# State-space scan: the rows of C by way of memory and a broadcasting transfer instead of a product and a copy

## The reference

```python
x_dbl = einsum('bld,ed->ble', x, W_xproj)          # 64 + 16 + 16 columns
dt_low, Bm, Cm = split(x_dbl, [64, 80])            # Bm, Cm: 16 values per token
delta = softplus(einsum('blr,dr->bld', dt_low, W_dt) + b_dt)
# for each of 256 channels d and 16 states n, along the 128 tokens t:
h[t, d, n] = exp(delta[t, d] * A[d, n]) * h[t-1, d, n] + delta[t, d] * x[t, d] * Bm[t, n]
y[t, d]    = sum_n h[t, d, n] * Cm[t, n]
x = layernorm(x + y)
```

## Time and profile before

| what | value |
|---|---|
| median of 3 runs | 1385.7 us (1383.73 to 1385.78) |
| profiled execution, its own time | 1390.1 us |
| span of the profiled execution | 1388.3 us |
| mean granted clock of TensorE | 0.929 of full |
| scan phase | from the start to about 522 us |
| VectorE busy from 30 to 507.3 us | 460.1 of 477.3 us |
| TensorE busy in the same stretch | 366.4 us |
| ScalarE | 298.5 us |
| GpSimd | 336.7 us |
| transfers in the same stretch | 2% of 16 DMA engines, 7 GB/s |

### The profile page before, as it was taken

How to read it: one execution, slowest core, us unless ns; L and a number is a source line. 1 busy time by engine, 2 the same in 40 slices (tenths; PEclk the granted TensorE clock), 3 DMA queues, 4 the chain that set the end, 5 groups by cost and what they waited for, 6 DMA issues and landing times. The chain is left out here.

```text
span 1388.3 us, 25930 instructions
## 1 busy us (share of the span) xinstructions
PE 1079.9 (78%) x8527; PEld 733.4 (53%) x8527; DVE 1000.8 (72%) x1898; ACT 751.8 (54%) x1601; POOL 794.1 (57%) x730
## 2 busy tenths in 40 slices
PE   5877778787777766888888888213999999999980
PEld 1332323233232224666666666103899989999970
DVE  2999999999999984787787776574455555555534
ACT  4666575666657624666667665202555555555433
POOL 2686776768677654777777775403144644454423
PEclk8999999999999997999999998556999999999995
DMA  3000000000000001111111100203134444434227
GB/s 108 16 16 1 16 0 15 1 15 15 0 1 0 1 0 33 37 35 42 38 34 43 38 31 33 77 0 110 55 66 108 97 104 72 107 84 79 42 22 254
DMA packets 43463, 64.01 MB, mean 46 GB/s; under 512 B 8288, under 2 KB 34592, under 8 KB 41248
## 3 DMA queue, kind: packets, MB, share of 16 engines
q1 hardware_dynamic: 31104, 46.11, 10.0%
q0 software_dynamic: 12288, 17.05, 7.5%
HBM read 42.00 MB, written 21.14 MB: 45 GB/s over the span
## 5 line engine op out<-in xcount | busy, mean ns | idle before, releaser
L514 POOL TENSOR_TENSOR scan_hc<-scan_state,scan_c_sb 128x1024 f32<-128x1024 f32 x128 | 305.4, 2391 | 142.8 <-DVE scan_state L442 132.9
L442 DVE TENSOR_TENSOR_SCAN scan_state<-scan_decay,scan_drive_ps 128x512 f32<-128x512 f32 x256 | 297.7, 1205 | 0.2
L223 PE MATMUL scan_y_ps<-scan_hc,all_ident 128*128 128x512 f32 x520 | 256.6, 617 | 3.1 <-POOL scan_hc L514 3.1
L1662 DVE TENSOR_TENSOR expert_hid_lo<-expert_hid,expert_hid_hi 128x512 fp32r<-128x512 f32 x128 | 88.6, 692 | 176.6 <-ACT expert_hid_hi L1646 163.4
L1559 POOL DMA_INDIRECT acc<-expert_rows,expert_lst x64 | 113.0, 1766 | 179.5 <-DVE expert_rows L1688 163.1
L1641 ACT ACTIVATE expert_hid<-expert_h_ps,expert_b 128x512 f32<-128x512 f32 x128 | 88.3, 690 | 199.0 <-PE expert_h_ps L556 175.8
L326 ACT ACTIVATE scan_decay<-scan_delta,scan_a_neg 128x508 f32<-128x508 f32 x256 | 169.6, 716 | 7.4 <-POOL scan_delta L496 7.2
L435 DVE TENSOR_TENSOR scan_drive_ps<-scan_dx,scan_b_ps 128x512 f32<-128x512 f32 x256 | 162.6, 681 | 14.3 <-POOL scan_dx L501 10.3
L368 ACT ACTIVATE scan_c_sb<-scan_c_ps 128x512 f32<-128x512 f32 x128 | 76.6, 599 | 138.7 <-PE scan_c_ps L216 129.6
L556 PE MATMUL expert_o_ps<-weights_w_hi,expert_hid_lo 128*128 128x256 f32 x512 | 143.2, 280 | 0.0
L223 PEld LDWEIGHTS scan_y_ps<-scan_hc,all_ident 128*128 128x128 f32 x520 | 99.8, 197 | 82.0 <-issue 72.7
(11 more groups left out here) (221 smaller groups left out, 2452.9 us busy)
## 6 DMA issues: line engine op xcount, KB each, us to landing
weights_w<-w SPq DMA_DIRECT2D x16, 1024.0 KB
table<-all_row SPq DMA_DIRECT2D x32, 132.0 KB, 1.8
scan_xT<-xT SPq DMA_DIRECT2D x8, 512.0 KB, 4.0
attn_ctxT<-ctxT SPq DMA_DIRECT2D x32, 128.0 KB, 2.4
acc<-all_row SPq DMA_DIRECT2D x32, 128.0 KB, 1.7
final_a<-acc SPq DMA_DIRECT2D x8, 512.0 KB, 6.5
out<-final_o SPq DMA_DIRECT2D x8, 512.0 KB, 4.2
expert_b<-b SPq DMA_DIRECT2D x8, 128.0 KB, 3.0
```

Source lines behind the costliest of these rows:

```text
L223: last = pe.matmul(y_ps[k][:], ident[0][:], hc[:, n % RING, k, :], start=False, stop=(n == NS - 1))
L442: dve.tensor_tensor_scan(state[:, n % RING, k, :], decay[:, n % RING, k, :, :].rearrange("p b t -> p (b t)"), drive_ps[k][:], 0.0, ALU.mul ...
L514: pool.tensor_tensor(hc[:, n % RING, :, :], state[:, n % RING, :, :], c_sb[:, n % RING, :].unsqueeze(1).broadcast_to([P, KH, GT]), ALU.mul ...
L1662: dve.tensor_tensor(hid_lo[:, f % RING_H, :], hid[:, f % 2, :], hid_hi[:, f % RING_H, :].bitcast(F32), ALU.subtract).then_inc(hid_ready, 1)
```

## The change

The rows of C are no longer spread by a product. ScalarE makes one more copy per group, of the 32 raw rows of B and C in fp32 (`c_rows`), directly behind the first bf16 part. SP stores C's 16 rows of 512 values (32 KB) to a buffer in memory, `c_dram`, one of two. Then for each step SP issues a transfer that reads one row of 2 KB and writes it to all 128 partitions of a slot of `c_sb` (256 KB), three steps ahead of the step that uses it. `broadcast_c`, its PSUM tile and ScalarE's copy are gone. GpSimd waits for the transfer, with a semaphore per slot of the ring. The semaphore `bc_high` is replaced by `c_rows_ready`, which comes after the fp32 copy, for both who waited for it: `split` on VectorE and `step_size` on TensorE. SP's program is written out by step, in a loop over pairs of groups: the store of the next group's rows stands at n = 12, and the load of xT moves to n = 14.

```diff
+                def store_rows(i, par):
+                    g = 2 * i + par
+                    sp.wait_ge(c_rows_ready, g + 1)
+                    sp.dma_start(c_dram[par], c_rows[NS:2 * NS, :]).then_inc(c_stored, 16)
+
+                def load_row(i, par, n):
+                    q = STEPS * (2 * i + par) + n
+                    if n == 0:
+                        sp.wait_ge(c_stored, 16 * (2 * i + par + 1))
+                    sp.wait_ge(hc_ready, q + 1)
+                    sp.dma_start(c_sb[:, n % RING, :], c_dram[par, n:n + 1, :].broadcast_to([P, GT])
+                                 ).then_inc(c_loaded[n % RING], 16)
+
+                def group(i, par, fetch, final=False):
+                    g = 2 * i + par
+                    for n in range(STEPS):
+                        if n == 12 and not final:
+                            store_rows(i + par, 1 - par)
+                        ahead = n + RING - 1
+                        if ahead < STEPS:
+                            load_row(i, par, ahead)
+                        elif not final:
+                            load_row(i + par, 1 - par, ahead - STEPS)
+                        if n == 14 and fetch:
+                            sp.wait_ge(y_started, g + 1)
+                            sp.wait_ge(dx_ready, g + 1)
+                            sp.dma_start(xT[par][:], xT_dram[:, :, ds((g + 2) * GT, GT)]).then_inc(x_loaded[par], 16)
...
                 def step_size(i, par):
-                    pe.wait_ge(bc_high, g + 1)
+                    pe.wait_ge(c_rows_ready, g + 1)
...
-                def broadcast_c(i, par, n):
-                    q = STEPS * (2 * i + par) + n
-                    pe.wait_ge(c_copied, q + 1)
-                    mm = pe.matmul(c_ps[:], sel[:, NS + n, :], bcs[par][:], start=True, stop=True)
-                    mm.then_inc(c_ready, 1)
...
                 def high_part(i, par, first=False):
                     if not first:
-                        act.wait_ge(c_ready, STEPS * (g - 1) + 1)
-                    act.activation(bcs[par][:], m_ps[1][0:96, :], ACT.Copy).then_inc(bc_high, 1)
+                        act.wait_ge(drive_ready, KH * STEPS * (g - 1) + 1)
+                    act.activation(bcs[par][:], m_ps[1][0:96, :], ACT.Copy)
+                    if not first:
+                        act.wait_ge(c_stored, 16 * g)
+                    act.activation(c_rows[:], m_ps[1][0:2 * NS, :], ACT.Copy).then_inc(c_rows_ready, 1)
...
-                        act.wait_ge(c_ready, q + 2)
-                        act.wait_ge(hc_ready, q + 1)
-                        act.activation(c_sb[:, n % RING, :], c_ps[:], ACT.Copy).then_inc(c_copied, 1)
...
                 def split(i, par):
-                    dve.wait_ge(bc_high, g + 1)
+                    dve.wait_ge(c_rows_ready, g + 1)
...
-                def outputs(q, n):
-                    pool.wait_ge(c_copied, q + 2)
+                def outputs(g, n):
+                    q = STEPS * g + n
+                    pool.wait_ge(c_loaded[n % RING], 16 * (STEPS // RING * g + n // RING + 1))
                     pool.wait_ge(scanned, KH * (q + 1 + RING))
                     pool.wait_ge(hc_summed, q + 1)
```

More of the change, by code:

```diff
@@ L69, in sem, with scan_phase @@
         return self.sems[-1]
-def scan_phase(nc, x1, ident, xT_dram, w_proj_dram, w_bc_dram, w_dt_dram, b_dt_dram, a_log_dram, sel_dram, attention):
+def scan_phase(nc, x1, ident, xT_dram, w_proj_dram, w_bc_dram, w_dt_dram, b_dt_dram, a_log_dram, sel_dram, c_dram, attention):
     with ExitStack() as ctx:
@@ L105, in scan_phase @@
         c_sb = s.sb("c_sb", [P, RING, GT])
+        c_rows = s.sb("c_rows", [2 * NS, GT])
         hc = s.sb("hc", [P, RING, KH, GT])
@@ L117, in scan_phase @@
         b_ps = s.ps("b", [P, 512])
-        c_ps = s.ps("c", [P, 512])
         drive_ps = [s.ps(f"drive{i}", [P, 512]) for i in range(KH)]
@@ L129, in scan_phase @@
         dt_copied = s.sem("dt_copied")
-        bc_high = s.sem("bc_high")
         bc_step = s.sem("bc_step")
@@ L141, in scan_phase @@
         b_ready = s.sem("b_ready")
-        c_ready = s.sem("c_ready")
-        c_copied = s.sem("c_copied")
+        c_rows_ready = s.sem("c_rows_ready")
+        c_stored = s.sem("c_stored")
+        c_loaded = [s.sem(f"c_loaded{i}") for i in range(RING)]
         drive_ready = s.sem("drive_ready")
@@ L174, in _ @@
                 attention.load(sp)
[L175 to L181, removed]
+                def store_rows(i, par):
[23 more added lines that the diff above has]
+                            sp.dma_start(xT[par][:], xT_dram[:, :, ds((g + 2) * GT, GT)]).then_inc(x_loaded[par], 16)
+                store_rows(0, 0)
+                for n in range(RING - 1):
+                    load_row(0, 0, n)
+                with sp.Fori(0, GROUPS // 2 - 1) as i:
+                    group(i, 0, True)
+                    group(i, 1, True)
+                group(GROUPS // 2 - 1, 0, False)
+                group(GROUPS // 2 - 1, 1, False, final=True)
             @block.tensor
@@ L252, in group @@
                         add_state(STEPS * g + n - 2, (n - 2) % STEPS)
-                        if ahead:
-                            broadcast_c(*ahead)
                         if n == 3:
@@ L261, in group @@
                                 step_size(i + par, 1 - par)
-                pe.sem_inc(c_ready, 1)
                 pe.wait_ge(proj_loaded, 16 * 2)
@@ L268, in _ @@
                 broadcast_b(0, 0, 0)
-                broadcast_c(0, 0, 0)
                 pe.wait_ge(zeroed, 3)
@@ L385, in group @@
                                 softplus_log(g + 1)
-                act.sem_inc(c_copied, 1)
                 act.sem_inc(turned, 1)
@@ L519, in group @@
                     for n in range(STEPS):
-                        outputs(STEPS * g + n, n)
+                        outputs(g, n)
                         if n == 5:
@@ L1812, in build @@
     acc = nc.dram_tensor("acc", (T, D), F32, kind="Internal").ap()
+    c_rows = nc.dram_tensor("c_rows", (2, NS, GT), F32, kind="Internal").ap()
     lists = nc.dram_tensor("lists", (EXPERTS, TOPK), I32, kind="Internal").ap()
@@ L1823, in build @@
             attention = AttentionConstants(Scope(nc, front, "xattn"), w_q, w_kv, w_o, w_g, norm, even_odd, pick)
-            scanned = scan_phase(nc, x1, (ident, ident_dram), xT, w_proj, w_bc, w_dt, b_dt, a_log, sel, attention)
+            scanned = scan_phase(nc, x1, (ident, ident_dram), xT, w_proj, w_bc, w_dt, b_dt, a_log, sel, c_rows, attention)
             attention_phase(nc, x1, ident, gate_all, attention, ctxT, table, acc, choice, row, row_stored, scanned)
```

## The result

| | before | changed |
|---|---|---|
| median of 18 runs | 1385.74 us | 1388.07 us |
| lowest and highest | 1383.73, 1388.96 | 1386.65, 1392.21 |
| span of the profiled execution | 1388.3 us | 1386.3 us |

The ratio is 1.0017, with a 95% interval from 1.0009 to 1.0025: 2.3 us slower, where +1.8 us was forecast. That is inside what counts here as the same, and inside the forecast's own range.

The account below looks back on a forecast made before the run. VectorE was taken to bound the scan at 3.42 us per step. Split delays of 7 x 0.18 = 1.3 us plus 0.5 us at the start gave +1.8 us, a median of 1387.5 us; range 1383 to 1394.

Parts of the forecast that it names:

- VectorE sets the pace of the scan, and C's product and copy are worth nothing in the step: Steady scan: the step stays 3.42 us on VectorE; removing 128 products and 128 ScalarE copies gains zero there.
- The fp32 copy in the way of the split: ScalarE, once per group: the added copy delays VectorE's split by 0.49 us, upper bound 0.59, paid in full.
- The projection 0.31 us earlier: TensorE, 7 groups: without the C product ahead, the projection starts 0.31 us earlier, bounds 0 and 0.38.
- The start: +0.49 us: Kernel start: the fp32 copy delays the chain to the first drive by 0.49 us, with no product removed ahead.
- The rows land in time: Row transfers to GpSimd: landing taken as 3.5 us against 11.2 us available, some 7 us spare, costing nothing.
- Traffic costs nothing, and the gaps at the back edges don't grow: DMA and VectorE's loop: 77 GB/s of rows costs nothing; the forecast adds nothing for the 1.1 us issue gaps.
- ScalarE's busy time 72 us less, TensorE's 50: Scan: expected drops in busy time, about 72 us on ScalarE and about 50 us on TensorE.
- The clock: TensorE: slow stretches at 1.2 GHz, perhaps more with fewer products, cost nothing where VectorE stays busy.
- The second rival: TensorE's projections run at 1.2 GHz: 12 to 24 us over 7 groups, 1399 to 1411 us; chance 0.07.
- The first rival, small delays that add up: Projection not earlier, copy costs 0.59: 4.7 us, 1390.4 us; back-edge gaps grow up to 7 us, giving 1394; chance 0.22.
- Its sign: VectorE: idle before the split exceeding 2.0 us would point to small delays adding up; that case's chance 0.22.
- The fourth rival's fast end, -1.6 us: Last state sum on TensorE may find the fast clock, -1.6 us; with the 1.3 us saved, 1384.6 us; chance 0.09.

Follow-up runs that it names:

- the later split: The kernel before with the split at n = 9 and the preparation steps behind it one step later; ratio 1.0013 of the kernel before.
- that of the second: The unaltered changed kernel measured once more against the kernel before; ratio 1.0028 (1.0018 to 1.0037), +3.9 us.
- The same edit: Split at n = 9, step sizes and middle parts n = 10, last part n = 11; kernel before 1.0013, changed kernel 0.9955, both against the kernel before.
- the two further edits: On the changed kernel with split at n = 9: b product between projection halves, bf16 and fp32 copies before the low part's; 0.9918, 1374.54 us.
- the cut projection: TensorE's projection halved around the next b product, run only with split at n = 9 and reordered copies on the changed kernel; 0.9918.

## Why the prediction was right

- **VectorE sets the pace of the scan, and C's product and copy are worth nothing in the step.** Right: the groups kept 1202 and 679 ns, and the product put back lengthens the waits of the split by 0.22 us each and nothing else that could be seen in the waits.
- **The fp32 copy in the way of the split: +0.49 us per group.** Right: 0.48, shown by adding it alone, and by moving it away.
- **The projection 0.31 us earlier.** Mis-sized: 0.22. The start of C's product and that of the projection stood 0.31 us apart, but 0.09 of it remains: C's product started 1.72 us behind the state sums, and without it the projection starts not 1.72 but 1.81 us behind them. Net 0.26 per group in place of 0.18, and 1.8 us in place of 1.3.
- **The start: +0.49 us.** 0.48 from the bf16 copy to the split. The first drive came at 27.64 and 25.37 us in the two executions of the kernel before, so that it could not be seen in the time; the forecast's 28.1 was not met (25.57), by chance.
- **The rows land in time.** Right: 3.1 us, between the 3.0 of the experts' bias and the 3.5 taken, with 11.2 available; with 4.4 us nothing measurable is lost, with about 1 us the whole landing is in the step. Three rows in flight, which the prediction allowed for, is not what happens: mostly it is one. The store landed in 2.9 us, not 1.8, and had room too.
- **Traffic costs nothing, and the gaps at the back edges don't grow.** Right for the changed kernel: 1.06 and 1.03 us, and 1.22 and 1.01, 1.33 and 1.01 in its other two executions, against 1.11 and 1.10.
- **ScalarE's busy time 72 us less, TensorE's 50.** Mis-sized: 62.6 and 30.7 in the scan. Nothing in the time hung on it.
- **The clock.** A slow stretch between groups costs nothing, as the earlier trace rows said. The second rival, set at 7%, had slow projections in every group. None of the 21 was slow, all took 1.93 us. What exists is smaller: a projection that is late behind slow sums, 0.83 us where it strikes, two groups of 21. What the Trainium skill says, "TensorE: Matmul & The Clock Gate", Part 1, that activity is what releases the clock, fits the slow stretches: the one of the earlier trace rows follows a pause of TensorE of 2.45 us. It does not settle the long ones: the kernel with the C product back had one as well (2.58 us), and so had the kernel before with the later split, so that fewer products alone are not shown to be their cause.
- **The first rival, small delays that add up.** Its mechanism was not seen: the projection was earlier, the copy cost 0.48 and not 0.59, the back edges stayed. Its sign, an idle of over 2.0 us ahead of the split, held in no group of the first profile, but in two of the second, 2.71 and 2.73, for another reason, the slow sums. Its upper end, 1394, is the forecast and the 7 us; with the 1390.4 of the sentence before it would be 1397.
- **The fourth rival's fast end, -1.6 us.** The last state sum did take 1.98 us, but so it did in the second execution of the kernel before. It is chance, not a gain of the change.

So the mechanism was right and the size a little low. The forecast's +1.8 us lies inside the interval of the first comparison (1.2 to 3.5 us) and under that of the second (2.5 to 5.1), and so does the trace's sum of 2.3. The delayed projections of that second execution, 2 x 0.83 = 1.7 us, would bring it to 4.0. An estimate from all five traces lies between: the scan was 482.1 us on average in three executions of the changed kernel and 479.7 in two of the kernel before, 2.4 us, and with the 0.48 of the start 2.9. How often the slow sums strike, and with it this part of the size, stays open.

What the freed engines are worth showed only with another order of the preparation. The same edit gives the kernel before nothing and the changed kernel some 9 us, and the two further edits bring that to some 14 us. Not all of it need be the change's: of the 10.7 us that the kernel before lost again, 5.8 stood behind the projection, and whether the cut projection would win them there as well was not tried.

## What to carry to other kernels

Here work taken off engines that wait anyway brought nothing by itself. What counted was the one short instruction that was put ahead of a waiting bottleneck engine, and it counted in full. Ask of each edit which in-order wait it lengthens, then look what order of the rest the freed engines would now allow. A row spread by a transfer is as good as a product and a copy where it can be asked for well over a landing ahead; 4.4 us were enough for 3.1. And read every wait of a total, not one example of it: the same 10.7 us held two causes.

## What the runs showed of the hardware

A transfer of 256 KB that reads one 2 KB row 128 times lands in 3.1 us when one is issued about every 3.4 us, and in 3.0 when one is issued about every 5.7. That is less than the 4.4 us of a 512 KB load that reads each byte once. At 76 GB/s into SBUF beside them the instructions of VectorE and GpSimd did not get longer: 1202 and 679 ns and 2381 ns, against 1205, 681 and 2391. In the kernel before and the changed one no stretch of 3.4 us near 1.2 GHz cost VectorE a wait. Of the longer ones ahead of a projection some cost 0.5 to 0.8 us and some less than 0.1. Not expected: a gap at the back edge of a loop that grew from about 1 to 3.2 us on VectorE when the order of the work of GpSimd and ScalarE was changed.
